# An attention layer over edges: three product blocks per slot instead of four, and one scale-and-add instruction per head for the running sums

## What is computed

```python
msg_s = (s_n @ Ws_src)[src] + (s_n @ Ws_dst)[dst]        # 64 scalars per edge
msg_v = (v_n . Wv_src)[src] + (v_n . Wv_dst)[dst]        # 32 vectors of 3
w1 = rbf @ W_rbf
m1_s, m1_v = _cg_tp(msg_s, msg_v, y0, y1, ...w1...)      # first product
a = (m1_s @ W_alpha).reshape(e, H, 16)
a = sum(leaky_relu(a) * alpha_dot)                        # one logit per head, 4 heads
alpha = softmax of a over the edges of the same dst
val_s = m1_s @ Ws_val
val_v = (m1_v . Wv_val) * sigmoid(val_s @ Wg)
val_s = sigmoid(val_s)
m2_s, m2_v = _cg_tp(val_s, val_v, y0, y1, ...w2...)      # second product
h = [m2_s @ Ws_vlin, m2_v . Wv_vlin]
agg = segment_sum(alpha * h, dst)
```

## Time and profile before

| what | us |
|---|---|
| median of 3 runs | 13186.02 |
| lowest, highest | 13185.72, 13264.55 |
| the profiled execution, whole | 13248.87 |
| its span, first to last instruction | 13246.9 |

### The profile page before, as it was taken

How to read it: one execution, slowest core, us unless ns; L and a number is a source line. 1 busy time by engine, 2 the same in 40 slices (tenths; PEclk the granted TensorE clock), 3 DMA queues, 4 the chain that set the end, 5 groups by cost and what they waited for, 6 DMA issues and landing times. The chain is left out here.

```text
span 13246.9 us, 282237 instructions
## 1 busy us (share of the span) xinstructions
PE 10905.0 (82%) x70500; PEld 7225.5 (55%) x70501; DVE 8435.5 (64%) x29911; ACT 4988.2 (38%) x15104; POOL 8742.7 (66%) x12926
## 2 busy tenths in 40 slices
PE   5454453588887999996999956599999999999998
PEld 2000000366664555554666622288888888888886
DVE  7555553499973334433332369588888888888886
ACT  0000000266541222221111100177777777777775
POOL 3777777466655567743777745277777777777775
PEclk9999999999987799985555568699999999999998
DMA  4101100133223233322333356100000000000000
GB/s 154 28 25 25 28 25 19 37 68 68 68 50 66 60 72 74 75 53 57 82 82 82 82 107 117 32 20 20 20 20 20 20 20 20 20 20 20 20 20 21
DMA packets 964724, 635.56 MB, mean 48 GB/s; under 512 B 702351, under 2 KB 886629, under 8 KB 960972
## 3 DMA queue, kind: packets, MB, share of 16 engines
q0 software_dynamic: 257120, 382.51, 11.7%
q1 hardware_dynamic: 691340, 204.27, 8.4%
q10 hardware_dynamic: 15776, 43.25, 0.8%
HBM read 543.06 MB, written 86.47 MB: 48 GB/s over the span
## 5 line engine op out<-in xcount | busy, mean ns | idle before, releaser
L1124 POOL DMA_INDIRECT l1s_node_rows<-node_table,l1s_edge_rows x1216 | 1236.0, 1016 | 655.1 <-issue 316.0
L1124 POOL DMA_INDIRECT l2s_node_rows<-node_table,l2s_edge_rows x1216 | 1152.5, 948 | 653.7 <-issue 351.8
L1209 PE MATMUL l1s_p_outer<-l1s_edge_by_node,l1s_node_rows 128*32 128x64 f32 (+2 forms) x14592 | 1248.9, 275 | 110.7 <-DMA l1s_node_rows<-node_table,l1s_edge_rows 94.0
L461 PE MATMUL rank<-onehot,lower_h 128*128 128x418 f16 x812 | 429.7, 529 | 1035.8 <-DVE onehot L437 966.2
L744 POOL DMA_INDIRECT l_source_rows<-node_table,l_edge_rows x928 | 939.8, 1013 | 437.3 <-issue 278.1
L1209 PE MATMUL l2s_p_outer<-l2s_edge_by_node,l2s_node_rows 128*64 128x40 f32 (+1 forms) x4864 | 1039.2, 345 | 152.8 <-DMA l2s_node_rows<-node_table,l2s_edge_rows 149.2
L1209 PEld LDWEIGHTS l2s_p_outer<-l2s_edge_by_node,l2s_node_rows 128*64 128x64 f32 (+1 forms) x4864 | 837.3, 233 | 549.9 <-issue 356.5
L1209 PEld LDWEIGHTS l1s_p_outer<-l1s_edge_by_node,l1s_node_rows 128*32 128x32 f32 (+2 forms) x14592 | 771.9, 132 | 668.9 <-issue 494.5
L474 POOL DMA_INDIRECT rows_by_src<-row_s,pos_i x812 | 846.6, 1043 | 416.4 <-issue 416.4
L1971 POOL DMA_INDIRECT l_source_rows<-node_table,l_edge_rows x914 | 891.1, 975 | 317.6 <-issue 244.4
L474 POOL DMA_INDIRECT rows_by_dst<-row_d,pos_i x812 | 845.0, 1041 | 267.3 <-issue 267.3
(11 more groups left out here) (504 smaller groups left out, 29142.2 us busy)
## 6 DMA issues: line engine op xcount, KB each, us to landing
l_xv_by<-h_turned_l SPq DMA_DIRECT2D x120, 320.0 KB, 10.6
l_source_rows<-node_table,l_edge_rows POOLq DMA_INDIRECT x1842
l_xs_by<-h_turned_l SPq DMA_DIRECT2D x40, 640.0 KB
rows_by_src<-pad_rows_s ACTq DMA_DIRECT2D x23, 1026.0 KB
l1s_edge_rows<-rows_by_src SPq DMA_DIRECT2D x304, 76.0 KB, 2.3
l2s_edge_rows<-rows_by_src SPq DMA_DIRECT2D x304, 76.0 KB, 2.5
l1s_node_rows<-node_table,l1s_edge_rows POOLq DMA_INDIRECT x1216
l2s_node_rows<-node_table,l2s_edge_rows POOLq DMA_INDIRECT x1216
```

The source lines that it names most:

```text
L461: nc.tensor.matmul(rank[:, b, 0:BINS], K["lower_h"][:, :], onehot[:, b, :], start=True, stop=False)
L1124: pool.indirect_dma_start(xg[q][:, s, :], None, table, bass.IndirectOffsetOnAxis(ap=pay[q][:, s, S_DST:S_DST + 1].bitcast(U32), axis=0)).t ...
L1209: ins = nc.tensor.matmul(p_o[rows, j % RING, col:col + n], xg[q][:, s, lhs], rhs(eh[q % RING][:, s, :, :]), start=True, stop=True, skip_gr ...
```

## The change

First and second product no longer carry `s*y1` per axis. Since `(s y1[i]) W = (s W) y1[i]`, three blocks per slot are enough: block 0 holds `s*y0` (64 columns) and the dot in two parts (its first two terms added, the third apart), the other 256 columns hold `s` once (64), `v*y0` (96) and the cross (96), for all axes. The values come out 128 columns wide, one `s` part and three axes; DVE multiplies the `s` part with y1 afterwards (`spread`) and adds it (`val_sum`), and likewise for the heads (`head_spread`, `head_sum`). PSUM is laid out anew: the sums per node share a bank with the values (`p_v`), the heads' scalar part with the logits (`p_a`), the heads' vector part with the turned products (`p_t`). The running sums become four `scalar_tensor_tensor` (scale, then add from PSUM) of 41 columns each, at the place of the old scaling. Weight loads: 56 instead of 40.

```diff
-        w_a, w_v = sb("w_a", [P, D]), sb("w_v", [P, 3, 3 * CV])
-        w_hs, w_hv = sb("w_hs", [P, CS]), sb("w_hv", [P, 3, HEADS, 3, AV])
+        w_a, w_v = sb("w_a", [P, D]), sb("w_v", [P, 2, P])
+        w_hs, w_hv = sb("w_hs", [P, CS]), sb("w_hv", [P, 2, P])
...
-            n_loads, LOADS = [], 40
+            n_loads, LOADS = [], 56
```

POOL keeps the y1 of the pair for the heads two turns later:

```diff
                             wait("val_made", t("val_made"))
+                            nc.gpsimd.tensor_copy(axis_kept[prev % 2][:, :, :], pay[prev][:, :, D_E4 + 1:D_E4 + 4])
```

PE: three blocks, two vector matmuls per slot, `acc_done` ahead of the values, `front_turn` ahead of the transposes of G, `tanh_done` ahead of the heads (and `val_made` ahead of the sums per node):

```diff
-                            for n in ("a_done", "a_scaled", "a_crossed"):
+                            for n in ("a_done", "a_crossed"):
                                 wait(n, -1)
-                            wait("g_copied", -1)
                             for s in range(PAIR):
-                                for c in range(4):
-                                    ins = nc.tensor.transpose(p_t[s][:, c * P:(c + 1) * P], F[prev % 2][:, s, c, :], K["ident"][:, :])
+                                for c in range(BLOCKS):
+                                    ins = nc.tensor.transpose(p_t[:, s, c * P:(c + 1) * P], F[prev % 2][:, s, c * P:(c + 1) * P], K["ident"][:, :])
                                 ins.then_inc(m["f_turned"], 1)
                             wait("max_taken", 0, 1)
                             masked(1, prev2)
-                            wait("val_made", -1)
+                            wait("acc_done")
                             for s in range(PAIR):
                                 wait("f_copied", 0, s + 1)
...
+                                nc.tensor.matmul(logits[:, s, :], f_t[s][:, 0:P], w_a[:, :], start=True, stop=True)
+                                for c in range(2):
+                                    ins = nc.tensor.matmul(values[:, s, :], f_t[s][:, (c + 1) * P:(c + 2) * P], w_v[:, c, :], start=c == 0, stop=c == 1)
                             ins.then_inc(m["logits_done"], 1)
+
+                            wait("a3_copied", -1)
+                            wait("hot_made")
+                            front_turn(ahead_u)
...
-                            wait("acc_done")
+                            wait("tanh_done")
                             for s in range(PAIR):
                                 wait("g_copied", 0, s + 1)
...
+                                nc.tensor.matmul(heads_s[:, s, :], g_t[s][:, 0:P], w_hs[:, :], start=True, stop=True)
+                                for c in range(2):
+                                    ins = nc.tensor.matmul(p_t[:, s, AT_HV:AT_HV + P], g_t[s][:, (c + 1) * P:(c + 2) * P], w_hv[:, c, :], start=c == 0, stop=c == 1)
```

ACT: the six `s*y1` pieces of F and of G go (in their place come one add that writes `s` into G and four pieces scaled by y0, after the exponentials); between the logits and the copies of the turned G its order is now:

```diff
                             wait("logits_done")
-                            wait("b_done", -1)
-                            nc.scalar.activation(slope[:, :, :], p_a[:, :, 0:CS], ACT.Copy, scale=0.2)
-                            nc.scalar.activation(th[:, :, :], p_a[:, :, CS:D], ACT.Tanh, scale=0.5).then_inc(m["tanh_done"], 1)
+                            wait("lsum_made", -1)
+                            nc.scalar.copy(alphas[:, :, :], logits[:, :, 0:CS]).then_inc(m["alphas_made"], 1)
+                            nc.scalar.activation(th[:, :, :], logits[:, :, CS:D], ACT.Tanh, scale=0.5).then_inc(m["tanh_done"], 1)
+                            wait("val_made", -1)
+                            wait("tanh_done")
+                            nc.scalar.add(gate[:, :, :], th[:, :, CS:MS], 1.0).then_inc(m["gate_made"], 1)
+                            wait("front_turned")
+                            wait("front_done", -1)
+                            front((u + 1) % 4)
                             wait("heads_done", -1)
                             for s in range(PAIR):
                                 wait("g_turned", 0, s + 1)
-                                nc.scalar.copy(g_t[s][:, :], p_t[s][:, :]).then_inc(m["g_copied"], 1)
+                                nc.scalar.copy(g_t[s][:, :], p_t[:, s, 0:PT]).then_inc(m["g_copied"], 1)
-                            wait("front_turned")
-                            wait("front_done", -1)
-                            front((u + 1) % 4)
```

`front` is two copies there, 256 and 128 wide; the bf16 copy of the one-hot comes later, from SBUF. DVE:

```diff
                             msg_made = w.done(TT(msg[:, :, :], p_r[:, :, AT_DST:AT_DST + D], xg[u][:, :, :], ALU.add))
+                            wait("summed", -1)
                             wait("shrink_done", -1)
                             wait("acc_done", -1)
-                            shrunk = w.done(TT(acc_b, acc_b, free(shrink[:, :], [1, HEADS], [0, HW]), ALU.mult))
+                            for h in range(HEADS):
+                                ins = nc.vector.scalar_tensor_tensor(acc_b[:, h, :], acc_b[:, h, :], shrink[:, h:h + 1], p_sum[:, h * HW:(h + 1) * HW], ALU.mult, ALU.add)
+                            ins.then_inc(m["acc_done"], 1)
+                            onehot((u + 1) % 4, it * 16 + 16 * ((u + 1) // 4 + 1))
...
                             TT(uv[:, :, 1, :, :], weight(2), msg_v, ALU.mult).then_inc(m["ux_made"], 1)
                             v_made = w.done(TT(uv[:, :, 0, :, :], weight(1), msg_v, ALU.mult))
+                            TT(f[:, :, AT_SV:AT_V], p_r[:, :, CS:2 * CS], msg[:, :, 0:CS], ALU.mult)
+                            TT(by_axis(f[:, :, AT_V:AT_X]), weight(0), msg_v, ALU.mult)
+                            TT(f[:, :, 0:CS], p_r[:, :, 0:CS], msg[:, :, 0:CS], ALU.mult).then_inc(m["uv_made"], 1)
 
                             wait("masked", -1, 2)
                             nc.vector.tensor_reduce(qm[:, 0:2], p_m[:, :, :], AX.X, ALU.max).then_inc(m["max_taken"], 1)
...
-                            wait("summed", -1)
-                            w.after(shrunk)
-                            TT(acc_b, acc_b, p_h[:, SUM:SUM + HEADS * HW].rearrange("p (h c) -> p h c", h=HEADS), ALU.add).then_inc(m["acc_done"], 1)
...
                             wait("heads_done")
-                            for s, done in ((0, "rows_used"), (1, "z_made")):
-                                TT(Z[:, s, :, 0:HW - 1], heads(s), free(Z[:, s, 0, HW - 1:HW], [HW, HEADS], [0, HW - 1]), ALU.mult).then_inc(m[done], 1)
...
+                            spread_made = w.done(TT(head_spread[:, :, :, :], free(p_t[:, 0, AT_HV:AT_HV + 1], [512, PAIR], [0, 3], [1, CV]),
+                                                    free(old[:, 0, 0:1], [3, PAIR], [1, 3], [0, CV]), ALU.mult))
...
+                            TT(Z[:, :, :, 0:AS], heads_s.rearrange("p s (h c) -> p s h c", h=HEADS), weigh([0, AS]), ALU.mult)
+                            w.after(spread_made)
+                            w.link(TT(head_sum[:, :, :, :], by_axis(head_v[:, :, CV:P]), head_spread[:, :, :, :], ALU.add))
+                            for s in range(PAIR):
+                                ins = TT(Z[:, s, :, AS:HW - 1].rearrange("p h (j c) -> p h j c", c=AV), head_sum[:, s, :, :].rearrange("p j (h c) -> p h j c", c=AV),
+                                         free(Z[:, s, 0, HW - 1:HW], [HW, HEADS], [0, 3], [0, AV]), ALU.mult)
+                            ins.then_inc(m["z_made"], 1)
```

More of the change, by code:

```diff
@@ L2174, in _ @@
                             nc.scalar.copy(a3_t[0:3 * HEADS, :], p_a3).then_inc(m["a3_copied"], 1)
-                            scale_b(1).then_inc(m["b_scaled"], 1)
+                            wait("val_made")
+                            for s in range(PAIR):
+                                ins = nc.scalar.activation(g[:, s, AT_V:AT_X], val_v[:, s, :, :].rearrange("p i c -> p (i c)"), ACT.Copy, scale=y0(s))
+                            ins.then_inc(m["b_scaled"], 1)
                 @block.vector
@@ L2179, in _ @@
                     v = Steps(dve, m["steps"])
-                    for group in (pay, xg, hot, hot_t, hot_tb, F, G_, logit, (a3, Z, acc, shrink, mn, ea, drop)):
+                    for group in (pay, xg, hot, hot_t, hot_tb, F, G_, logit, axis_kept, (a3, Z, acc, shrink, mn, ea, drop)):
                         for tile in group:
@@ L2262, in _ @@
-                            w.after(dropped)
-                            dve.sem_inc(m["dve_seen"], 1)
-                            nc.vector.tensor_copy(top_b, mn[:, :]).then_inc(m["max_made"], 1)
-                            wait("tanh_done")
-                            leaky_made = w.done(TT(leaky[:, :, :], p_a[:, :, 0:CS], slope[:, :, :], ALU.max))
-                            wait("b_scaled", -1)
-                            nc.vector.tensor_scalar(sg[:, :, :], th[:, :, :], 1.0, None, ALU.add).then_inc(m["sg_made"], 1)
+                            TT(f[:, :, AT_D:MS], dots[:, :, 0, :], dots[:, :, 1, :], ALU.add).then_inc(m["a_done"], 1)
@@ L2270, in _ @@
+                            spread_made = w.done(TT(spread[:, :, :, :], free(p_v[:, 0:1], [P, PAIR], [0, 3], [1, CV]), y1(prev, [1, 3], [0, CV]), ALU.mult))
                             wait("a3_made", -1)
@@ L2282, in _ @@
```

(7 more changed lines are left out.)

190 lines of the change are left out of this document (97 added, 93 removed).

## The result

The changed kernel takes 14,170.28 us (median of four, 14,138 to 14,192), beside 13,187.35 for the kernel before on the same chip: a ratio of 1.073, 95% interval 1.068 to 1.077. I had forecast slower, 13,560, at most 13,880. The direction was right; the size was 2.7 times what I had summed.

A forecast was written before the change was run, and what follows sets the result against it. PE's own list bounds the loop; the new order makes PE wait for DVE, so a turn goes from 10.01 to 10.81 us: 0.80 x 456 = 365, + 8 = 373 us on 13,186, say 13,560; range 13,200 to 13,880.

The forecast's parts named there:

- The path to the first maximum: DVE from sums through scale-and-adds, one-hot and five products: maximum ends at 3.80 us, PE idles 1.8 us before masked(1).
- PE's blocks: PE's own work at prices per record: 128-wide 0.12 us, values 1.56, G's transposes with waits 0.71, heads 1.50.
- ACT's copy: Copy of turned G, now behind ACT's front copies, stalls PE 0.28 us ahead of the heads.
- The heads' chain: DVE's instructions from the last heads record to z_made: end at 10.70 us, 10.75 with the hop to PE.
- it just fits: DVE's work behind the heads reaches PE at 10.75 us, under PE's own 10.81; the old 0.8 us slack is used up.
- the rival I had given 14%: DVE's work behind the heads ends the turn, POOL possibly slowing it: 11.3 to 11.8 us, 13,790 to 14,010 us; 14%.
- The clock: Rival: PE's clock falls to 1.2 GHz in new idle time, 15,000 us or above; 3% together with table loads.
- The other half of that rival: ACT's gate add brings a table load into each turn: 13,800 us or above; 3% together with the clock falling.
- 0.80 predicted: Growth of the loop's turn from 10.01 to 10.81 us, x 456 turns = 365 us.
- The 8 us that I had added for sixteen more weight loads: Sixteen more loads in SP's queue delay DVE's wait for all of them: 8 us taken, 9.6 at most.
- My fastest rival: PE's list stays the bound: 8.71 us a turn, 12,600 us; 6%, together with anything between that and -1%.
- busy about as long as before: DVE's added products, 0.26 us each, stand against what goes, so DVE's busy time stays about the same.

The follow-up runs named there:

- e2: Changed kernel with DVE's bin-register loads put back behind the second product: ratio 1.055 to the kernel before, 12.08 us a turn.
- e12: Changed kernel in its own order, next bins loaded in one go behind the second maximum into a second register set: 14,023 us, ratio 1.064 to the kernel before.
- e3: Changed kernel with 16 useless transposes in PE's wait for DVE's first maximum: ratio 1.032 to the kernel before, 11.27 us a turn.
- e1: Changed kernel with DVE's wait for the sums, scale-and-adds and one-hot moved behind the first maximum: ratio 0.999 to the kernel before, 10.21 us a turn.
- e7: Changed kernel with running sums and one-hot behind the first maximum and bin registers loaded after the second product: 13,456 us, ratio 1.019 to the kernel before.
- e10: e1 with both bin registers loaded by one instruction of three words: 13,290 us, ratio 1.008 to the kernel before.
- e13: Kernel before, bins loaded in one go behind the second maximum into a second register set: 13,322 us, ratio 1.010 to the unaltered kernel before.
- e11: Changed kernel, sums behind first maximum, G copied first, one three-word load behind the second maximum into a second register set: 13,075 us, ratio 0.988 to the kernel before.

## Why the prediction was wrong in size

**The path to the first maximum: right.** By the full-clock turn (t from 10,023.84): scale-and-adds from 0.94 (0.86 predicted), four in 0.68 until the one-hot (0.64), one-hot done 2.06 (1.94), the five products exactly 1.19, maximum ends 3.93 (3.80), masked(1) at 4.08 (3.95). The scale-and-adds, which no row of before showed, lay between the bounds at 0.17 each. That agrees with the 0.168 us that the Trainium skill's "VectorE: DVE Perf Modes" (the section on the TRN2 errata) gives for 41 columns out of PSUM. PE's idle stretch is 2.19 us, predicted 1.8, as PE's six transposes were done at 1.89, not 2.1.

**PE's blocks: right, a bit dear.** A 128-wide record takes 0.11, not 0.12: values 1.43 (1.56), G's transposes 0.65 (0.71), heads 1.51 (1.50).

**ACT's copy: right place, 0.51 instead of 0.28.** ACT starts at t = 6.14, to the hundredth as predicted. Its gate add and front copies end 0.05 later, PE's maxima come 0.07 earlier, and the hop from ACT's copy to PE is 0.15, where I had put 0.04. The same that gave me 0.15 for the hop behind the maximum would have given it here. Up to the front, PE's list is thus 0.17 late: its logit parts would end at 10.98 instead of 10.81.

**The heads' chain: "it just fits" failed.** It was to end at 10.75 and let the sums start; they start at 11.24. The chain starts 0.17 later with the rest, its last two multiplies take 0.61 instead of 0.40, and the hop is 0.15 where I had put 0.05. That is the mechanism of the rival I had given 14%, at 0.26 us a turn, just short of its 11.3 to 11.8. The rival named POOL as a possible cause, and the trace of the changed kernel supports it. Its 912 last multiplies take 0.25 us on average where no arithmetic of POOL on tensors overlaps them (137) and 0.37 where one overlaps at least half of them (775); the three instructions of the chain that read PSUM keep their times although POOL overlaps nearly all of them (L2323: 0.34 to 0.35 us each time). The Trainium skill's "GPSIMD Engine Reference" (Key points) has DVE and POOL share their interfaces to SBUF, with contention for DVE instructions with two SBUF inputs; that is the same division. No run took POOL away, so it is a correlation, if a strong one.

**The register loads: not in my sum at all.** The change moves them, and the prediction doesn't name them. The move cost nothing (e2). The loads themselves do, at either place: in a full-clock turn DVE waits for the heads anyway (0.32 us, behind the pause), in the turns with the lower clock it doesn't. Hiding them gives back 5,507 - 5,379 = 128 us in e12, 0.28 a turn; that is a part of the slow turns' lateness and not to be added to the clock's price below.

**The clock: the step that failed.** "Against: layer 0 has PE 89% busy with gaps and holds 1.00", hence 3%, and nothing in the sum. Layer 0 was the wrong row: from 2600 to 3800 its longest gap is 0.9 us, not 2.2 us in each turn, and after the change PE is busy 76%. The clock fell, though not for good: to 1.2 GHz for some 3.4 us, and in 55% of the turns. I had also priced it as lasting (15,000 or above). e3 gives its price, 0.83 us a turn, some 380 us of the 610 by which the sum was short. The other half of that rival did not happen: ACT loads a table once in four turns (114 times in the loop), before and after.

Together: 0.80 predicted + 0.17 PE's path + 0.26 heads' chain + 0.86 from the full-clock turn's 11.24 to the mean of 12.10 = 2.09 us a turn. The first three terms reach 11.24 by construction, and the last is a difference; what checks it independently is e3, with 11.27 measured at full clock. The 8 us that I had added for sixteen more weight loads can't be seen: outside the loop the changed kernel took 13 us less in one pair of profiles and 13 more in the other.

Two things stay open. Why are nearly half of the turns spared? Neighbours with the same idle stretch fall on either side. And which property of the stretch matters, its length or PE's share? Another layer of this same program shows that neither alone is a safe sign (the kernel before; the row has the same order as the earlier trace rows):

```profile
7000.00:7500.00 500.00, 462.96 (x1848) 307.74 (x1847) 153.27 (x999) 88.84 (x400) 378.24 (x400) 0.50 0.37 82
```

PE is 93% busy there and has the lower clock throughout; but for one of 3.2 us, no idle stretch of its is longer than 0.7 us.

**And where did PE's saved 1.17 us go?** My fastest rival, PE staying the bound at 8.71, came true in no order tried. With the sums behind the maximum the turn is 10.21, DVE's 9.2 us of work plus its pause and short waits. I had called DVE "busy about as long as before". That was the second weak point: it was busy 8.35 us a turn before, 8.9 in the changed kernel and 9.2 in e1, and the pause comes on top. Three instructions with both inputs in SBUF stand behind the rise. In the changed kernel they take 0.42, 0.29 and 0.29 us on average; in e1 they are 0.80 us longer together, while others are shorter or overlap more (12,000 to 15,000; count, busy us, mean ns of one):

```profile
L2224 DVE TENSOR_TENSOR l_node_onehot<-iota_f,l_edge_rows 128x256 f32<-128x256 f32 x294 | 189.1, 643 | 0.0
L2270 DVE TENSOR_TENSOR l_dot_parts<-l_weighted_v,l_edge_rows 128x128 f32<-128x128 f32 x294 | 191.5, 651 | 0.0
L2271 DVE TENSOR_TENSOR l_product<-l_weighted_v,l_edge_rows 128x64 f32<-128x64 f32 x294 | 146.6, 499 | 0.0
```

In e1 they stand where POOL multiplies too: the nine times that no arithmetic of POOL overlapped L2270, it took 0.28 us. As long as PE's list was 10 us long all this was harmless; it is what the orders tried met once PE's was shorter.

## What to carry to other kernels

An instruction that waits for TensorE must not stand on another engine ahead of the one that TensorE itself waits for: here that order, with the clock that fell in its wake, was 863 us of the 956 lost. Before trusting a saving on the bound engine, add up the next engine's list with its pauses, since that is the new turn: with PE 1.17 us lighter only 0.33 could be had, and only after a 0.6 us register load had been hidden. When you weigh whether the clock will hold, don't take the average busy share of another layer for an answer: look also at the longest idle stretch in the inner turn, and if the clock falls, try filling or moving that stretch, as e3 and e1 did.

## What the chip showed that I had not expected

- TensorE's granted clock fell to 1.2 GHz for some 3.4 us in 55% of the turns. PE was idle for 2.2 us in every turn and busy 76%; useless transposes in that stretch brought the mean clock from 0.92 to 1.00 and 0.83 us a turn back. Other runs with PE less busy than before kept 1.00 (e7: 83%, its longest wait 0.9 us).
- A register load of one word takes VectorE's sequencer 0.31 us, one of three words 0.75, and the next instruction in the engine's list starts only after it, while those ahead of it still run. What shows of that depends on what the engine still has to do meanwhile: a pause of 0.6 us in e1 and e10, 0.28 in e13, none in e11.
- Four scale-and-adds of 41 columns with a per-partition scale take 0.17 us each in a row, though one by itself lasts 0.25; two 164-wide instructions for the same work changed the turn by 0.05.
- The same VectorE instruction with all its inputs in SBUF can take more than twice as long beside GpSimd's arithmetic: 0.65 us instead of 0.28 for a 128-wide product in e1. Instructions that read PSUM kept their times.
